# A graph network's node stages: two interleaved groups of tiles set half a chain apart

## Chip, core and metric

The kernel runs on one core of a Trainium2 chip. The metric is the device time of one execution in microseconds, lower is better; the median of three runs stands for a kernel. An engine (TensorE, VectorE, ScalarE, GpSimd, and SyncE for transfers) works through its own list of instructions in order; semaphores order the engines among each other.

## What is computed

A network of four layers on a graph of 6250 nodes and 100,000 edges. Each node has 64 scalars and 32 vectors of three components, 160 numbers. Each layer sends messages over the edges, sums them at the nodes, and ends with

```python
x = _layernorm(x + _L0_gnn_ref(x, ...), axis=-1)     # and so for layers 1, 2, 3
```

What a node does in between is small: projections of its 64 scalars and 96 vector components with small matrices, layer norms (mean, variance, `(variance + eps) ** -0.5`), a gate, in layer 0 a feed-forward part, and in layer 3 `cos(angle) * sc + sin(angle) * conv`. At the end of a layer the node's features are multiplied into the table (`tab_src`, and `tab_dst` for layers 0 and 2) from which the next layer's edges gather.

## The kernel before

The nodes are padded to 7168, or 56 tiles of 128. A *group* is `G = 4` tiles. `node_phase(nc, W, D, post, pre)` (line 2024) is the node stage between two edge stages: it ends layer `post` and prepares the tables of layer `pre`. It is called five times, with (None, 0), (0, 1), (1, 2), (2, 3) and (3, None); the edge stages (not touched) lie between. Each call loops `PAIRS = 7` times over two groups, `both`, which have their own buffers, PSUM and semaphores (`class Group`, line 1987). One pass of the loop is called a round here.

The work on a group is one chain: the list `stages` names its L steps in order (L is 12, 46, 35, 22 and 33 in the five calls), and the semaphore `B.done` counts them. A step waits until the step before it of the same group is done, whichever engine did that:

```python
def at(eng, name, B, j):
    eng.wait_ge(B.done, 1 + j * L + index[name])
```

On every engine each step is issued `for B in both`, that is for group 0 and then for group 1, before the next step. So the two groups go through the chain together, one step's length apart. In the steps, `turn_...` are transposes on TensorE (L2151, L2210), `move_...` copy their result out of PSUM on ScalarE (L2255, L2256), `product`, `f1`, `f2`, `tables` are matmuls (L2158, L2223, L2225), `..._mean` to `..._norm` is a layer norm, of which the step `..._root` is a power on GpSimd (L2137) and the rest is on VectorE, with the square on ScalarE. `move_t` writes the table's tile, `pair` takes the sums that the edge stage left.

In the calls (None, 0) and (0, 1) GpSimd has a second task, off the chain: it raises the edges' squared lengths, W["norm"], 784 columns, to the power -0.5, a seventh of them (112 columns) at the end of each round (L2142).

SyncE loads the sums of a group for the next round once the step `used` (`turn_a` or `move_v`) is reached, and stores tables or output when a group's chain is whole. There is one buffer of each kind for a group.

Of the kernel before, what the change touches and what calls it, by code (L numbers as in the profile page):

```python
# [17 lines left out]
ALU = mybir.AluOpType  # L18
# [3 lines left out]
P = 128  # L22
# [4 lines left out]
G = 4  # L27
PAIRS = -(-N_NODES // (P * 2 * G))
NT = PAIRS * 2 * G
# [332 lines left out]
def edge_tables(nc, W, D):  # L362
# [3 lines left out]
    with ExitStack() as ctx:  # L366
# [14 lines left out]
        GROUPS = ET // 16  # L381
        BATCH = 4
        batches = [range(a, min(a + BATCH, GROUPS)) for a in range(0, GROUPS, BATCH)]
# [1640 lines left out]
def node_phase(nc, W, D, post, pre):  # L2024
# [49 lines left out]
    with ExitStack() as ctx:  # L2074
        S = Names(nc, ctx, f"n{post}{pre}".replace("None", "x"))
        sem = S.sem
        both = [Group(S, n, post, pre, n_tab, H) for n in range(2)]
        X = lambda B, j: W["x"][:, bass.ds((j * 2 + B.n) * G, G), :]
        NA = lambda B, j: W["na"][:, bass.ds((j * 2 + B.n) * G, G)]
# [6 lines left out]

        @block.sync
        def _(sp):
            def load(B, j):
                if post == 1:  # L2090
                    for k in range(TM):
                        sp.dma_start(B.ag[k][:, :, :], rows(D["acc"][post][k][0:NPAD, :], j * 2 + B.n)).then_inc(B.loaded, 16)
                else:

                    for t in range(G):
                        slot = sp.value_load(W["last"][0:1, bass.ds((j * 2 + B.n) * G + t, 1)], min_val=0, max_val=V)
                        sp.dma_start(B.ag[0][:, t, :], D["sums"][post][bass.ds(slot, 1), :, :].rearrange("o p c -> (o p) c")).then_inc(B.loaded, 16)

            def store(B, j):

                if pre is not None:
                    for n, name in enumerate(("tab_src", "tab_dst")[0:n_tab]):
                        sp.dma_start(rows(D[name], j * 2 + B.n), B.tab[:, n, :, :]).then_inc(B.stored, 16)
                else:
                    sp.dma_start(rows(D["out"], j * 2 + B.n), B.final[:, :, :]).then_inc(B.stored, 16)
# [8 lines left out]
            with sp.Fori(1, PAIRS) as j:  # L2114
                if post is not None:
                    for B in both:

                        wait_apart(sp, B.done, 1 + (j - 1) * L + index[used], sem("sp_passed"))
                        load(B, j)
                for B in both:  # L2120

                    wait_apart(sp, B.done, 1 + j * L, sem("sp_passed"))
                    store(B, j - 1)
            for B in both:
                sp.wait_ge(B.done, 1 + PAIRS * L)
                store(B, PAIRS - 1)
# [3 lines left out]
        @block.gpsimd  # L2130
        def _(pool):
            with pool.Fori(0, PAIRS) as j:  # L2132
                for tag in ("ln2_", "end_", "pre_"):
                    if tag + "root" in index:
                        for B in both:
                            at(pool, tag + "root", B, j)
                            nc.gpsimd.tensor_tensor(B.st[:, :, :], B.st[:, :, :], W["half"][:, 0:2 * G].rearrange("p (a t) -> p a t", a=2), ALU.pow)\  # L2137
                                .then_inc(B.done, 1)
                if norms is not None:

                    share = norms[:, bass.ds(j * (ET // PAIRS), ET // PAIRS)]
                    nc.gpsimd.tensor_tensor(share, share, W["half"][:, 0:ET // PAIRS], ALU.pow).then_inc(sem("norms"), 1)  # L2142

        @block.tensor
        def _(pe):
# [19 lines left out]
            pe.wait_ge(sem("ones"), 2)  # L2165
            with pe.Fori(0, PAIRS) as j:
                if post in (0, 2):
                    for B in both:
# [3 lines left out]
                    for B in both:  # L2172
# [6 lines left out]
                if post == 0:  # L2179
                    for B in both:  # L2180
# [3 lines left out]
                    for B in both:  # L2184
# [3 lines left out]
                    for B in both:  # L2188
# [4 lines left out]
                    for B in both:  # L2193
# [3 lines left out]
                if post in (1, 3):  # L2197
                    per = 128 if post == 1 else 96
                    for B in both:
# [3 lines left out]
                    for B in both:  # L2203
# [3 lines left out]
                    for B in both:  # L2207
# [5 lines left out]
                    if post == 1:  # L2213

                        for B in both:
                            at(pe, "product", B, j)
                            times(B.wideB, 0, (B.aT[:, :], W["l1_out_s"][:, :]), (B.sT[0:64, :], W["l1_skip_s"][:, :])).then_inc(B.done, 1)
                        for B in both:
# [9 lines left out]
                    else:  # L2228

                        for B in both:  # L2230
# [5 lines left out]
                        for B in both:  # L2236
# [3 lines left out]
                if pre is not None:  # L2240
                    for B in both:
                        src = B.nrm if pre in (0, 2) else B.out
                        at(pe, "turn_p", B, j)
                        turn(src, 0, C0, B.psA)
                        turn(src, C0, CX, B.psA, SECOND).then_inc(B.done, 1)
                    for B in both:
                        at(pe, "tables", B, j)
                        times(B.wideB, 0, (B.sT[0:W[f"l{pre}_tab_s"].shape[0], :], W[f"l{pre}_tab_s"][:, :]))
                        times(B.wideA, 0, (B.vT[:, :], W[f"l{pre}_tab_v"][:, :])).then_inc(B.done, 1)

        @block.scalar
        def _(act):
# [5 lines left out]
            def square(tag, source, j):  # L2258
                for B in both:
                    src = source(B)  # L2260
                    at(act, tag + "square", B, j)
# [3 lines left out]
            with act.Fori(0, PAIRS) as j:  # L2265
                if post in (0, 2):
                    for B in both:
# [3 lines left out]
                if post == 0:  # L2271
                    square("ln2_", lambda B: B.res, j)
                    for B in both:
# [3 lines left out]
                    for B in both:  # L2277
# [5 lines left out]
                    for B in both:  # L2283
# [4 lines left out]
                    for B in both:  # L2288
# [4 lines left out]
                    for B in both:  # L2293
# [4 lines left out]
                if post in (1, 3):  # L2298
                    per = 128 if post == 1 else 96
                    for B in both:  # L2300
# [3 lines left out]
                    for B in both:  # L2304
# [3 lines left out]
                    for B in both:  # L2308
# [3 lines left out]
                if post == 1:  # L2312
                    for B in both:
                        at(act, "silu", B, j)
                        nc.scalar.activation(B.out[:, :, 0:C0], B.wideB[:, :, 0:C0], ACT.Silu).then_inc(B.done, 1)
                    for B in both:
                        at(act, "gate_t", B, j)
                        nc.scalar.activation(B.th[:, :, :], B.wideB[:, :, C0:96], ACT.Tanh, scale=0.5).then_inc(B.done, 1)
                if post == 3:

                    for B in both:
                        at(act, "sine", B, j)
                        nc.scalar.activation(B.whole_t[:, :, :], B.ang[:, :, :], ACT.Sin).then_inc(B.done, 1)
                if post is not None:
                    for B in both:
                        at(act, "end_square", B, j)
                        nc.scalar.activation(B.sqr[:, :, :], B.cen[:, :, :], ACT.Square).then_inc(B.done, 1)  # L2327
                if pre in (0, 2):
                    square("pre_", lambda B: B.out, j)
                if pre is not None:  # L2330
                    for B in both:
# [11 lines left out]
                    for B in both:  # L2343
# [6 lines left out]
                        last.then_inc(B.done, 1)  # L2350

        @block.vector
        def _(dve):
# [9 lines left out]
            def stats_eq(tag, source, j, dv, eps):  # L2363

                scalars, vectors = lambda B: source(B)[:, :, 0:C0], lambda B: source(B)[:, :, C0:CX]
                for B in both:
                    at(dve, tag + "mean", B, j)
                    reduce(B.st[:, 0, :], scalars(B)).then_inc(B.done, 1)
                for B in both:
                    at(dve, tag + "scale_mean", B, j)  # L2370
                    ts(B.st[:, 0, :], B.st[:, 0, :], -1.0 / C0, None, ALU.mult).then_inc(B.done, 1)
                for B in both:
                    at(dve, tag + "centre", B, j)
                    tt(B.cen[:, :, 0:C0], scalars(B), bcast(B.st[:, 0, :], 2, C0), ALU.add).then_inc(B.done, 1)
                for B in both:
# [3 lines left out]
                for B in both:  # L2379
# [3 lines left out]
                for B in both:  # L2383
# [6 lines left out]
            with dve.Fori(0, PAIRS) as j:  # L2390
                if post is not None:
                    for B in both:
# [6 lines left out]
                    if post == 1:  # L2399
                        for B in both:  # L2400
                            at(dve, "sum", B, j)
                            tt(B.ag[0][:, :, :], B.ag[0][:, :, :], B.ag[2][:, :, :], ALU.add).then_inc(B.done, 1)
                if post in (0, 2):
                    total = lambda B: B.ag[0][:, :, CX:CX + H]
                    for B in both:
                        at(dve, "denom", B, j)
                        ts(B.den[:, :, :], total(B), 1e-12 if post == 0 else 1e-16, None, ALU.add).then_inc(B.done, 1)
                    for B in both:
                        at(dve, "recip", B, j)
                        nc.vector.reciprocal(B.den[:, :, :], B.den[:, :, :]).then_inc(B.done, 1)  # L2410
                    if post == 0:
                        for B in both:
                            at(dve, "ratio", B, j)
                            tt(B.ratio[:, :, :], total(B), B.den[:, :, :], ALU.mult).then_inc(B.done, 1)
                    for B in both:
# [5 lines left out]
                if post == 0:  # L2421

                    for B in both:
# [3 lines left out]
                    for B in both:  # L2427
                        at(dve, "merged", B, j)
                        tt(B.nrm[:, :, 0:C0], B.nrm[:, :, 0:C0], B.cen[:, :, 0:C0], ALU.add).then_inc(B.done, 1)
                if post == 0:  # L2430
                    for B in both:
                        at(dve, "residual", B, j)
                        tt(B.res[:, :, :], X(B, j), B.wideB[:, :, 0:CX], ALU.add).then_inc(B.done, 1)
                    stats_eq("ln2_", lambda B: B.res, j, C1V, 1e-5)
                    for B in both:
# [3 lines left out]
                    for B in both:  # L2439
# [5 lines left out]
                    for B in both:  # L2445
# [3 lines left out]
                    for B in both:  # L2449
# [3 lines left out]
                    for B in both:  # L2453
                        at(dve, "both", B, j)
                        tt(B.out[:, :, :], B.out[:, :, :], B.res[:, :, :], ALU.add).then_inc(B.done, 1)
                    for B in both:
                        at(dve, "whole", B, j)
                        tt(B.res[:, :, :], B.out[:, :, :], X(B, j), ALU.add).then_inc(B.done, 1)
                if post == 1:
                    for B in both:  # L2460
                        at(dve, "gate_half", B, j)
                        ts(B.th[:, :, :], B.th[:, :, :], 0.5, 0.5, ALU.mult, ALU.add).then_inc(B.done, 1)
                    for B in both:
                        at(dve, "gated", B, j)
                        tt(comp(B.out[:, :, C0:CX]), comp(B.wideA[:, :, 0:C1V]), bcast(B.th[:, :, :], 2, 3), ALU.mult).then_inc(B.done, 1)
                    for B in both:
                        at(dve, "whole", B, j)
                        tt(B.res[:, :, :], B.res[:, :, :], B.out[:, :, :], ALU.add).then_inc(B.done, 1)
                if post == 2:

                    for B in both:
                        at(dve, "twice", B, j)
                        tt(B.out[:, :, :], B.res[:, :, :], B.wideB[:, :, 0:CX], ALU.add).then_inc(B.done, 1)
                    for B in both:
                        at(dve, "whole", B, j)
                        tt(B.res[:, :, :], B.res[:, :, :], B.out[:, :, :], ALU.add).then_inc(B.done, 1)
                if post == 3:
                    for B in both:
# [3 lines left out]
                    for B in both:  # L2482
# [3 lines left out]
                    for B in both:  # L2486
                        at(dve, "turns", B, j)
                        ts(B.whole_t[:, 0, :], B.ang[:, 0, :], 1.0 / (2 * PI), None, ALU.mult).then_inc(B.done, 1)
                    for B in both:
                        at(dve, "turns_i", B, j)  # L2490
                        nc.vector.tensor_copy(B.turns_i[:, 0, :], B.whole_t[:, 0, :]).then_inc(B.done, 1)
                    for B in both:
                        at(dve, "turns_f", B, j)
                        nc.vector.tensor_copy(B.whole_t[:, 0, :], B.turns_i[:, 0, :]).then_inc(B.done, 1)
                    for B in both:
# [11 lines left out]
                    for B in both:  # L2507
# [170 lines left out]
```

## Time and profile before

| | |
|---|---|
| time, three runs | 13734.82 us median (13729.59 to 13742.96) |
| the profiled execution | 13737.42 us, of which 13735.7 us from the first to the last instruction |
| TensorE, VectorE, GpSimd, ScalarE busy | 76%, 64%, 59%, 34% of the span |
| granted clock of TensorE, mean | 0.761 of 2.4 GHz |
| the five node stages (us from the start) | about 166 to 323, 3805 to 4370, 6960 to 7460, 11170 to 11415, 13397 to 13735 |

The page of the profile cuts the span into 40 slices of 343 us; a digit is a share in tenths. Line numbers (L2142) are those of the code above. A timeline row gives the start, the length from the first of its instructions to the end of the last, the engine, the line, what is written and read, and how many instructions (x8); an f32 matmul of this kernel shows as two. In brackets stands how long the engine was idle before it, and what ended that.

### The profile page before, as it was taken

What the parts mean: (1) busy time and instruction counts of PE and PEld (TensorE: products, weight loads), DVE (VectorE), ACT (ScalarE), POOL (GpSimd) and SP (SyncE); (2) the same over time, 40 slices, a digit from 0 to 9 for tenths busy, and PEclk for the clock granted to TensorE, in tenths of its full rate; (3) what the DMA queues carried; (4) which work ended last, traced back from release to release, by engine and by line L of the source; (5) the groups of instructions that cost most, each with busy time, mean ns of one, the idle gap of its engine ahead of it and who ended that gap; (6) DMA issues with size and microseconds to landing.
All of it is one profiled execution on the core that took longest, in us unless ns stands there. A gap on an engine that the chain in (4) does not pass through costs nothing. (4 is left out here: it accounts for less than half of the span.)

```text
span 13735.7 us, 242376 instructions
## 1 busy us (share of the span) xinstructions
PE 10467.3 (76%) x54203; PEld 8391.8 (61%) x54203; DVE 8817.4 (64%) x21902; ACT 4716.7 (34%) x11245; POOL 8106.9 (59%) x8692
## 2 busy tenths in 40 slices
PE   2999999937756666666655999999976767888885
PEld 2888888836654222222245999999975655555554
DVE  4677777775534555555534999999985445555553
ACT  1555555500022222222212777777750002222221
POOL 4788888825524888888822666666635534555540
PEclk7788888855556777777766999999975557888885
DMA  3454544424402888888852222222214532222221
GB/s 93 107 114 113 115 114 114 109 64 129 129 24 46 132 132 131 132 131 132 132 150 83 74 74 74 74 74 75 75 47 119 125 80 61 69 69 69 69 68 46
DMA packets 1339115, 1294.01 MB, mean 94 GB/s; under 512 B 504078, under 2 KB 1142018, under 8 KB 1338374
## 3 DMA queue, kind: packets, MB, share of 16 engines
q0 software_dynamic: 347904, 594.12, 23.4%
q1 hardware_dynamic: 913612, 653.03, 17.8%
q10 hardware_dynamic: 77498, 45.68, 1.1%
q8 instruction: 43, 0.70, 0.0%
q14 instruction: 58, 0.48, 0.0%
HBM read 781.38 MB, written 510.73 MB: 94 GB/s over the span
## 5 line engine op out<-in xcount | busy, mean ns | idle before, releaser
L625 POOL DMA_INDIRECT e_gs<-tab_src,e_ix x1568 | 1731.9, 1105 | 926.8 <-DMA e_ix<-in_dst 506.3
L625 POOL DMA_INDIRECT e_gd<-tab_dst,e_ix x1568 | 1620.6, 1034 | 478.0 <-issue 478.0
L676 PE MATMUL e_psS<-e_rows,e_same 128*128 128x480 f32 x1568 | 1120.1, 881 | 847.1 <-DVE e_same L650 847.1
L1391 PE MATMUL s_psS<-s_wv,s_hot 128*128 128x168 f32 (+1 forms) x3904 | 1183.0, 481 | 639.9 <-POOL s_wv L1349 357.8
L1602 POOL DMA_INDIRECT e_g<-tab_src,e_er x976 | 940.0, 963 | 963.6 <-DVE e_rows L1698 665.1
L1391 PEld LDWEIGHTS s_psS<-s_wv,s_hot 128*128 128x128 f32 x3904 | 1003.7, 316 | 818.6 <-issue 624.0
L694 POOL DMA_INDIRECT acc<-e_sums,e_row x784 | 1249.5, 1594 | 239.0 <-issue 209.7
L676 PEld LDWEIGHTS e_psS<-e_rows,e_same 128*128 128x128 f32 x1568 | 432.9, 294 | 1541.6 <-issue 1513.8
L581 PE MATMUL e_psF<-w_ident,e_F 128*128 128x128 f32 x7056 | 1343.0, 304 | 15.7 <-ACT e_FT L602 10.4
L608 ACT ACTIVATE e_O<-e_psO 128x352 f32<-128x352 f32 (+1 forms) x2352 | 1050.2, 447 | 768.6 <-PE e_psO L594 742.4
L602 ACT ACTIVATE e_FT<-e_psF 128x384 f32<-128x384 f32 x2352 | 1147.2, 488 | 307.4 <-PE e_psF L581 271.7
L581 PEld LDWEIGHTS e_psF<-w_ident,e_F 128*128 128x128 f32 x7056 | 938.6, 162 | 112.1 <-issue 56.6
L625 POOL DMA_INDIRECT e_g<-tab_src,e_ix x784 | 820.6, 1047 | 249.2 <-issue 175.2
L684 ACT ACTIVATE e_sums<-e_psS 128x480 f32<-128x480 f32 x784 | 447.8, 571 | 1509.7 <-PE e_psS L676 1509.7
L1626 PE MATMUL e_psS<-e_rows,e_hot 128*128 128x384 f32 x1952 | 941.0, 641 | 21.9 <-DVE e_hot L1700 12.3
L1347 POOL TENSOR_TENSOR s_wv<-s_val,s_pb 128x128 f32<-128x128 f32 x1464 | 776.8, 557 | 0.0
L1343 POOL TENSOR_TENSOR s_rel<-s_key,w_shift 128x4 int32<-128x4 int32 x488 | 98.0, 201 | 1142.1 <-DMA s_pb<-probs 1142.0
L2137 POOL TENSOR_TENSOR n_st<-n_st,w_half 128x8 f32<-128x8 f32 x70 | 113.4, 1638 | 1085.1 <-DVE n_st L2562 938.7
L593 PE MATMUL e_psO<-w_l_t,e_FT 128*128 128x128 f32 x3136 | 725.9, 317 | 0.0
L2255 ACT ACTIVATE n_sT<-n_psA 64x512 f32<-64x512 f32 x70 | 41.4, 591 | 1962.2 <-PE n_psA L2151 1960.9
L1626 PEld LDWEIGHTS e_psS<-e_rows,e_hot 128*128 128x128 f32 x1952 | 471.8, 254 | 360.5 <-issue 251.7
L591 PE MATMUL e_psO<-w_l_t,e_FT 96*128 96x128 f32 x3136 | 684.4, 304 | 2.0 <-ACT e_O L608 1.1
(481 smaller groups left out, 26530.6 us busy)
## 6 DMA issues: line engine op xcount, KB each, us to landing
s_val<-val SPq DMA_DIRECT2D x488, 320.0 KB
val<-e_O SPq DMA_DIRECT2D x392, 320.0 KB, 2.7
acc<-w_zeros SPq DMA_DIRECT2D x392, 139.5 KB
n_ag<-acc SPq DMA_DIRECT2D x56, 960.0 KB
e_krow<-in_src_t SPq DMA_DIRECT2D x196, 256.0 KB
sums<-e_total SPq DMA_DIRECT2D x244, 192.0 KB, 1.9
e_es<-in_es SPq DMA_DIRECT2D x196, 130.0 KB
e_gs<-tab_src,e_ix POOLq DMA_INDIRECT x1568
```

Source lines behind the costliest of these rows:

```text
L581: last = nc.tensor.transpose(psF[:, P * g:P * g + P], F[:, k, P * g:P * g + P], ident[:, :])
L591: nc.tensor.matmul(o[:, 0:scalars], f[0:96, 0:P], W[w + "_t0"][:, :], start=True, stop=True, skip_group_check=True)
L593: nc.tensor.matmul(o[:, x0:x0 + P], f[:, P:2 * P], W[w + "_t1"][:, :], start=False, stop=True, skip_group_check=True)
L602: nc.scalar.activation(FT[:, k, :], psF[:, 0:F_W], ACT.Copy).then_inc(S.sem(tag + "_FT"), 1)
L608: nc.scalar.activation(O[:, k, :], o[:, 0:width], ACT.Copy).then_inc(S.sem(tag + "_O"), 1)
L625: pool.indirect_dma_start(into[t][u][:, k, :], None, tables[t], bass.IndirectOffsetOnAxis(ix[u][:, t, k:k + 1], 0))\
L676: nc.tensor.matmul(psS[(k) % len(psS)], T["same"][u][:, k, :], values[:, k, :], start=True, stop=True)\
L694: pool.indirect_dma_start(acc[k], bass.IndirectOffsetOnAxis(T["row"][u][:, k:k + 1], 0), T["sums"][u][:, k, :], None, compute_op=ALU.add). ...
L1347: tt(wv[u][:, :, a:a + C1].rearrange("p t (h c) -> p t h c", h=H), val[u][:, :, a:a + C1].rearrange("p t (h c) -> p t h c", h=H), bcast(pb ...
L1391: last = nc.tensor.matmul(psS[u][:, 0:width], hot[u][:, k, :], wv[u][:, k, :], start=(k == 0), stop=(k == TM - 1))
L1602: pool.indirect_dma_start(g[u][:, k, :], None, D["tab_src"], bass.IndirectOffsetOnAxis(er[u][:, k, 12:13].bitcast(I32), 0))\
L1626: last = nc.tensor.matmul(psS[u % 2][:, 0:width], hot[u % 2][:, k, :], rows[u % 2][:, k, :], start=(k == 0), stop=(k == TM - 1))
```

## The change

All five calls. The two groups still alternate, but group 1 runs half a chain (`L // 2` steps) behind group 0. Each engine's list is written by `weave`: a step with index k of group B is put in slot `k + B.n * L // GROUPS`, taken modulo L, where the steps that overrun belong to the round before; in a slot, group 0 comes first. Steps that have no partner are peeled in front of the loop and behind it. The steps themselves, their waits and their buffers are the same. The power of W["norm"] is cut in smaller pieces, one behind each `root` step: 2 pieces of 56 columns a round in (None, 0), 4 of 28 columns in (0, 1). SyncE's list is put in the new order of events: for each group store (`whole`), then load (`free`).

```diff
+        offsets = [B.n * L // GROUPS for B in both]
+        def weave(eng, stream):
+            def turn(j, early, late):
+                runs = []
+                for B, offset in zip(both, offsets):
+                    runs += [[stream(B, j - 1), offset - L]] * early + [[stream(B, j), offset]] * late
+                for run in runs:
+                    run.append(next(run[0], None))
+                    while run[2] is not None and index[run[2]] + run[1] < 0:
+                        run[2] = step(run[0], False)
+                for slot in range(L):
+                    for run in runs:
+                        while run[2] is not None and index[run[2]] + run[1] == slot:
+                            run[2] = step(run[0], True)
...
+            turn(0, False, True)
+            with eng.Fori(1, PAIRS) as j:
+                turn(j, True, True)
+            turn(PAIRS, True, False)
...
-                        for B in both:
-                            at(pool, tag + "root", B, j)
...
-                    share = norms[:, bass.ds(j * (ET // PAIRS), ET // PAIRS)]
-                    nc.gpsimd.tensor_tensor(share, share, W["half"][:, 0:ET // PAIRS], ALU.pow).then_inc(sem("norms"), 1)
+            roots = [tag + "root" for tag in ("ln2_", "end_", "pre_") if tag + "root" in index]
+            share = ET // PAIRS // (len(roots) * GROUPS)
+            def stream(B, j):
+                for n, root in enumerate(roots):
+                    if (yield root):
+                        at(pool, root, B, j)
...
+                        if norms is not None:
+                            part = norms[:, bass.ds(((j * len(roots) + n) * GROUPS + B.n) * share, share)]
+                            nc.gpsimd.tensor_tensor(part, part, W["half"][:, 0:share], ALU.pow).then_inc(sem("norms"), 1)
+            weave(pool, stream)
...
-            with pe.Fori(0, PAIRS) as j:
+            def stream(B, j):
                 if post in (0, 2):
-                    for B in both:
+                    if (yield "turn_a"):
                         at(pe, "turn_a", B, j)
...
+            def free(B, j):
+                wait_apart(sp, B.done, 1 + j * L + index[used], sem("sp_passed"))
+                load(B, j + 1)
+            def whole(B, j):
+                wait_apart(sp, B.done, 1 + (j + 1) * L, sem("sp_passed"))
+                store(B, j)
...
+            with sp.Fori(1, PAIRS - 1) as j:
+                for B in both:
+                    whole(B, j - 1)
+                    if post is not None:
+                        free(B, j)
```

ScalarE's and VectorE's lists are rewritten as TensorE's is.

## Rows read from the trace of the kernel before

**Rows 1.** The page: span, and TensorE's busy tenths and granted clock by slices

```profile
span 13735.7 us, 242376 instructions
...
PE   2999999937756666666655999999976767888885
...
PEclk7788888855556777777766999999975557888885
```

**Rows 2.** Windows of one steady round in each of the five calls

```profile
core 0: us, PE busy (x) PEld busy (x) DVE busy (x) ACT busy (x) POOL busy (x), PEclk, DMA share, GB/s
172.30:193.80 21.50, 8.45 (x48) 7.48 (x48) 6.70 (x22) 7.09 (x16) 21.43 (x3) 0.66 0.20 61
3884.40:3963.70 79.30, 46.61 (x219) 40.96 (x218) 29.19 (x77) 20.96 (x52) 24.72 (x6) 0.59 0.06 17
7099.30:7170.30 71.00, 40.02 (x194) 34.96 (x193) 29.43 (x49) 16.14 (x34) 6.47 (x4) 0.59 0.36 129
11271.70:11306.25 34.55, 19.70 (x96) 17.20 (x96) 16.04 (x38) 7.29 (x14) 3.24 (x2) 0.55 0.14 39
13494.50:13539.80 45.30, 23.89 (x144) 22.34 (x144) 17.67 (x60) 8.13 (x16) 3.24 (x2) 0.61 0.17 50
```

**Rows 3.** Timeline of a round of (0, 1): single steps

```profile
3883.41 18.26 POOL L2142 TENSOR_TENSOR w_norm<-w_norm,w_half 128x112 f32 x1
...
3887.22 1.97 PE L2158 MATMUL n_psB<-w_l_tab_s,n_sT 64*128 64x64 f32 x8
...
3903.57 1.04 PE L2158 MATMUL n_psB<-w_l_proj_s,n_sT 65*128 65x64 f32 x8
...
3912.18 3.24 POOL L2137 TENSOR_TENSOR n_st<-n_st,w_half 128x8 f32<-128x8 f32 x2 [10.50 <-DVE n_st L2382]
...
3921.00 2.77 PE L2158 MATMUL n_psA<-w_l_f_v,n_vT 96*128 96x192 f32 x8
...
3924.18 1.15 ACT L2280 ACTIVATE n_sc<-n_psB,n_attr 128x128 f32<-128x128 f32 x4 [4.31 <-DVE n_attr L2438]
...
3930.32 1.77 ACT L2286 ACTIVATE n_th<-n_psB,n_attr 128x64 f32<-128x64 f32 x8
3931.89 2.69 ACT L2291 ACTIVATE n_fv<-n_psA,n_attr 128x192 f32<-128x192 f32 x8
3933.36 1.10 DVE L2443 SCALAR_TENSOR_TENSOR n_fv<-n_th,n_fv 128x256 f32<-128x256 f32 x3 [4.10 <-ACT n_fv L2291]
...
3943.23 0.42 DVE L2447 TENSOR_TENSOR n_out<-n_psB,w_l_f_b 128x256 f32<-128x256 f32 x1 [7.52 <-PE n_psB L2158]
...
3949.25 0.42 DVE L2447 TENSOR_TENSOR n_out<-n_psB,w_l_f_b 128x256 f32<-128x256 f32 x1 [5.14 <-PE n_psB L2158]
...
3950.06 1.55 DVE L2451 TENSOR_TENSOR n_out<-n_out,n_attr 128x640 f32<-128x640 f32 x2
...
3962.87 3.69 PE L2151 MATMUL n_psA<-w_ident,n_out 128*64 128x128 f32 x16 [13.65 <-DVE w_x L2571]
...
3964.79 0.59 ACT L2255 ACTIVATE n_sT<-n_psA 64x512 f32<-64x512 f32 x1 [6.33 <-PE n_psA L2151]
```

**Rows 4.** Timeline of a round of (1, 2): `pair`, and where `product` and `product_v` start

```profile
7099.28 2.16 DVE L2396 TENSOR_TENSOR n_ag<-n_ag 128x1920 f32<-128x1920 f32 x1 [6.35 <-ACT n_tab L2349]
...
7103.43 0.48 DVE L2398 COPY n_res<-w_x 128x640 f32 x1
...
7122.81 0.74 PE L2158 MATMUL n_psB<-w_l_out_s,n_aT 96*128 96x96 f32 x2
...
7128.17 0.74 PE L2223 MATMUL n_psA<-w_l_skip_v,n_vT 96*128 96x96 f32 x2
...
7135.02 0.72 PE L2223 MATMUL n_psA<-w_l_skip_v,n_vT 96*128 96x96 f32 x2
```

**Rows 5.** Timeline of a round of (3, None): the 24 small matmuls of `product`

```profile
13507.58 4.47 PE L2158 MATMUL n3x_psB<-w_l_w_v,n3x_gT 96*128 96x32 f32 x24
```

**Rows 6.** The instructions that write `w_norm`: count, shortest, median, longest in ns

```profile
L2142 POOL TENSOR_TENSOR w_norm<-w_norm,w_half x14: 18254/18258/18276, 175.6 to 4354.6; 128x112 f32 x14
```

More of the change, by code:

```diff
@@ L2113, in _ @@
                     load(B, 0)
-            with sp.Fori(1, PAIRS) as j:
-                if post is not None:
-                    for B in both:
-                        wait_apart(sp, B.done, 1 + (j - 1) * L + index[used], sem("sp_passed"))
-                        load(B, j)
-                for B in both:
-                    wait_apart(sp, B.done, 1 + j * L, sem("sp_passed"))
-                    store(B, j - 1)
-            for B in both:
-                sp.wait_ge(B.done, 1 + PAIRS * L)
-                store(B, PAIRS - 1)
+            def free(B, j):
[5 more added lines that the diff above has]
+            if post is not None:
+                for B in both:
+                    free(B, 0)
+            with sp.Fori(1, PAIRS - 1) as j:
+                for B in both:
+                    whole(B, j - 1)
+                    if post is not None:
+                        free(B, j)
+            for j in (PAIRS - 2, PAIRS - 1):
+                for B in both:
+                    whole(B, j)
             for B in both:
@@ L2228, in _ @@
                     else:
-                        for B in both:
+                        if (yield "product"):
                             at(pe, "product", B, j)
@@ L2271, in _ @@
                 if post == 0:
-                    square("ln2_", lambda B: B.res, j)
-                    for B in both:
+                    yield from square("ln2_", lambda B: B.res, B, j)
+                    if (yield "move_n"):
                         at(act, "move_n", B, j)
@@ L2328, in _ @@
                 if pre in (0, 2):
-                    square("pre_", lambda B: B.out, j)
+                    yield from square("pre_", lambda B: B.out, B, j)
                 if pre is not None:
-                    for B in both:
+                    if (yield "move_p"):
                         at(act, "move_p", B, j)
@@ L2389, in _, with stream @@
                 nc.vector.memset(B.sT[64:65, :], 1.0).then_inc(sem("ones"), 1)
-            with dve.Fori(0, PAIRS) as j:
+            def stream(B, j):
                 if post is not None:
-                    for B in both:
+                    if (yield "pair"):
                         at(dve, "pair", B, j)
@@ L2477, in _ @@
                 if post == 3:
-                    for B in both:
+                    if (yield "angle"):
                         at(dve, "angle", B, j)
```

206 lines of the change are left out of this document (104 added, 102 removed).

## Prediction

> **What bounds the kernel now.** The page first: one core, 13735.7 us from first to last instruction; the run that was profiled took 13737.42 us, 2.6 us above the median of the three timed runs (13734.82), so a difference worked out from the trace may be set on either. No engine is busy throughout, and the kernel is a row of stages. The change touches only the five calls of the node stage, so I looked for them in the instructions of the tiles `st`, `res` and `tab`, and then walked one steady round of each call in the timeline: a round is one pass of the loop over `PAIRS`, with two groups, and there are seven. The windows of one round each [rows 2] give everything: 21.5 us for the call before layer 0, 79.3 for (0, 1), 71.0 for (1, 2), 34.55 for (2, 3) and 45.3 for (3, None), together 251.65 us; seven times that is 1761 us, 12.8% of the kernel. The rest should not move.
>
> In four of the five rounds no engine is full: TensorE is busy 46.6 of 79.3 us, 40.0 of 71.0, 19.7 of 34.55 and 23.9 of 45.3 [rows 2]. These rounds are bound by the chain of dependent steps of a group, of which the other group hides a part. The exception is the first: GpSimd is busy 21.43 of 21.50 us. It raises 112 columns of `norms` to the power -0.5 each round, 18.26 us [rows 6], plus two `root` steps in 3.24 [rows 3].
>
> **Prices.** A step is taken as its duration plus 0.04 us where it follows on its own engine and about 0.1 where another engine hands over. VectorE over 640 columns: two groups in 1.55, so 0.86 alone. ScalarE: a move is two activations of 0.59, 1.2 with the handover; `scalars` 1.25, `gate_t` 0.95 and `gate_v` 1.4 (half of 1.77 and 2.69), `gated` 1.15. TensorE at its lower level (1.2 GHz): a `turn` 1.9 (two groups in 3.69), 8 matmuls of 64 columns 1.97, 8 of 192 columns 2.77, so `product` and `tables` of (0, 1) 3.95, `f1` 5.2; at the upper level (2.4 GHz) 1.04 in place of 1.97; `f2` 6.1 (its second group lies between 3943.2 and 3949.25) [all rows 3]. In (1, 2) `pair` is 4.65, `product` 5.4, `product_v` 6.9 [rows 4]; in (3, None) `product` is 1.97 + 4.47 = 6.4 [rows 3, 5]. With these, one chain alone at the lower clock is 60.5 us in (0, 1), 52.6 in (1, 2), 27.1 in (2, 3), 33.3 in (3, None).
>
> **What the change adds and moves.** No arithmetic goes or comes, apart from the cut of the `norms` power. Each engine's list is now in slots: group 0 is at stage k while group 1 is at k + L/2. All four engines work their lists in order, so an instruction of one group stands behind the one that the other has in an earlier slot, however late that is. Half a chain in *number of stages* puts these together. X is the group in the first half of its chain, Y the one in the second.
>
> (0, 1), L = 46, offset 23. Y: `scalars` to `f2` in slots 0 to 6 takes 1.25 + 0.95 + 1.4 + 1.15 + 2.9 + 1.6 + 6.1 = 15.35 us, in which X has only seven small VectorE steps (about 3 us). X's `turn_a` is slot 7, behind `f2` on TensorE: + 1.95 + 1.2 + 3.95, at 22.45. Both then stand in the statistics, on VectorE and ScalarE together: X's variance at 28.5. Both roots are in slot 17 (index 17 and 40): X's root 1.65, then the new piece of `norms` of 28 columns, then Y's root 1.65. The piece is priced by the slope between 8 columns in 1.64 and 112 in 18.26, 0.16 a column and 0.36 fixed: 4.85 us, put between the two roots; Y's root ends at 36.65. Y's `norm` 1.7 and `turn_p` 1.95: 40.3. X's `f1` is slot 21 and Y's `turn_p` slot 19 of one TensorE list, so `f1`, ready at 34.5, starts at 40.3 and ends at 45.4; Y's `tables` 3.9 and `move_t` 1.0: 50.3. X's `scalars` is slot 23, behind `move_t` on ScalarE. With the order inside a slot reversed (group 1 in the first half) the same walk gives 48.7. A round is 99.0 us at the lower clock.
>
> The clock gives some back. All TensorE work of this round at the lower level is 2 x 28.1 = 56.2 us (three turns 5.7, `product` 3.95, `f1` 5.2, `turn_f` 3.2, `f2` 6.1, `tables` 3.95); the trace has 46.6 [rows 2], so the upper level saved 9.6. I keep 85% of that, because TensorE's steps hold most, not all, of the new path: 99.0 - 8.2 = 90.8, a half of 45.4. The ends run alone: group 0's first half and group 1's second, together 60.5, 57 with the same share of clock. So 57 + 13 x 45.4 = 647 against 7 x 79.3 = 555: **+92**. Of it 7 x 9.7 = 68 us are the `norms` pieces, two a round on the path. They were hidden: the 18.26 us ran behind `end_root`, with no root wanted until the next `ln2_root`, 29 us after their start [rows 3].
>
> (1, 2), L = 35, offset 17. `pair` to `gate_half` of X is 4.65 + 2.15 + 3 x (2.0 + 1.2) + 5.4 + 6.9 + 1.1 = 29.8. Y has reached `pre_norm` at about 20, but that is slot 12 on VectorE behind X's `gate_half`; only then `norm` 1.0, `turn_p` 1.95, `move_p` 1.45, `tables` 4.8, `move_t` 1.7: 40.7. The other half is alike, 81.4 a round. Two chains of TensorE steps at the lower level (four turns 7.8, 5.4, 6.9, 4.8) are 49.8, the trace has 40.0 [rows 2]: the clock saves 9.8 now, 85% kept: 73.1. With ends of 50: 50 + 13 x 36.55 = 525 against 497: **+28**.
>
> (2, 3), L = 22, offset 11: X's `share` ready at 4.0 (behind Y's `sum`), `turn_a` 2.05, `move_a` 1.2, `product` 3.95, then Y's `turn_p` behind `product` on TensorE 1.95, `move_p` 1.2, `tables` 3.95, `move_t` and `tab_attr` 1.8: 20.1, or 40.1 a round; less 0.85 x (23.4 - 19.7) is 37.0. 26 + 13 x 18.5 = 266 against 242: **+24**.
>
> (3, None), L = 33, offset 16: X to the end of `product_v` 0.5 + 6.0 + 3.6 + 6.4 + 3.9 = 20.4; Y's `scale` stands behind X's `angle`, and its `centre`, `square`, `sum`, `var`, root and `norm` add 6.0: 26.4, or 52.8; less 0.85 x (32.6 - 23.9) is 45.4. 31 + 13 x 22.7 = 326 against 317: **+9**.
>
> First call: GpSimd still bounds. Two pieces of 56 columns cost one fixed part of 0.36 us more than one of 112: 7 x 0.36, **+3**.
>
> SyncE: the same loads and stores in the order in which they fall due (whole of group 0, its `used`, whole of group 1, its `used`). Each load is issued when its buffer is free, most of a chain ahead, so I cost it at nothing; were the loads of (1, 2) late, VectorE's `pair` would show it.
>
> Sum: 3 + 92 + 28 + 24 + 9 = +156 us, **13,890 us** (+1.1%).
>
> **A rule beside the rows.** What the clock will grant is the least certain term. In the page's slices TensorE's nines come with a granted 7 to 9, yet the rounds here, busy 59, 56, 57 and 53%, were granted 0.59, 0.59, 0.55 and 0.61 [rows 1, 2]. The Trainium skill ("TensorE: Matmul & The Clock Gate", Part 1) says that the clock rises with sustained work and falls back when the engine idles, and that such oscillation costs a kernel whose bursts are broken by waits. By that rule the change, which cuts the bursts of two groups into single ones, would push the clock down, and the sum would be nearer the first rival; by the rows it stays at 0.55 to 0.6.
>
> **The rivals.**
> 1. *The clock stays at its lower level* in the four calls. Then nothing is given back, at the ends neither (60.5 + 13 x 49.5 = 704 in (0, 1), and so on): 704 + 582 + 288 + 376.5 + 153.5 against 1761 is +343, 14,078 us. For it: single bursts; against: the share granted hardly varies over four different rounds. 0.15.
> 2. *The clock rises*, since some TensorE work is now nearly always there. At the upper level throughout, each half loses half its TensorE time: 36.55, 28.2, 14.1 and 18.2 us; with ends of 46.5, 40, 21 and 25 the sums are 522, 407, 204 and 262, and with the 153.5 of the first call -212, 13,523 us. It decides from the point where 343 of the 555 us between these two levels are given back, 62% of the work at the upper level; it is 32 to 53% now. 0.16, of which 0.08 ends within 0.2% of no change.
> 3. *The order doesn't bind* and the two chains overlap as in the idea: each call then takes seven and a half single chains, 454 + 395 + 203 + 250 = 1302 against 1611, and +3 in the first: 13,429 us. For it: TensorE and VectorE are free enough. Against: the slots above; it needs that two long TensorE steps don't meet. 0.08.
> 4. The forecast, 0.61, with a range of its own of 13,800 to 14,000 (the 85% taken as 50 to 100%, the `norms` piece costing half of what the slope says or all, and 0.1 us a handover either way).
>
> **Range and chances.** 13,740 to 14,080 leaves out rival 3 and the faster half of rival 2. Beyond 0.2% (27 us; closer than that this kernel's runs can't be told apart) faster: 0.08 + 0.08 = 0.16; within: 0.08; slower: 0.61 + 0.15 = 0.76.
>
> **What would show it.** Rounds of about 91, 73, 37 and 45 us in the timeline, GpSimd full in the first call with 9.3 us pieces; in (0, 1) the second root 6.5 us after the first, and `f1` released by nothing but the place behind `turn_p`; in (1, 2) VectorE idle before `pre_norm` until ScalarE's `gate_t`, long after its root. The granted clock of each call tells 1 and 2 apart from 4. I am wrong if rounds come near 65, 55, 30 and 36 us (the order doesn't bind), or if the time is made in another stage.

## The result

The changed kernel takes 14064.76 us, median of four runs (14042.80 to 14074.75); the kernel before took 13738.89 us in the four runs beside it. The ratio is 1.0233, with a 95% interval of 1.0215 to 1.0250: slower by 326 us, 2.4%. The forecast was slower by 156 us, 13,890, in a range up to 14,080. The direction and most of the mechanism held; the size is off by a factor of two, and it was off in one term. The first rival (TensorE's clock stays at its lower level) had put 14,078 us on it.

The profiled execution of the changed kernel spans 14041.1 us, 305.4 more than before. First, where: the windows of the whole node stages, each from the first to the last instruction of its call, in the order (None, 0), (0, 1), (1, 2), (2, 3), (3, None). Before:

```profile
core 0: us, PE busy (x) PEld busy (x) DVE busy (x) ACT busy (x) POOL busy (x), PEclk, DMA share, GB/s
165.80:322.70 156.90, 66.09 (x336) 58.72 (x336) 47.10 (x142) 49.66 (x112) 150.06 (x21) 0.61 0.19 58
3807.20:4373.50 566.30, 321.22 (x1512) 282.70 (x1512) 205.18 (x534) 147.12 (x364) 172.90 (x35) 0.58 0.06 17
6942.50:7456.60 514.10, 276.09 (x1344) 242.54 (x1344) 207.24 (x338) 112.30 (x238) 45.37 (x28) 0.60 0.35 125
11160.30:11413.00 252.70, 135.14 (x672) 118.10 (x672) 113.47 (x254) 51.00 (x98) 22.71 (x14) 0.55 0.13 37
13391.30:13734.90 343.60, 182.10 (x1008) 170.70 (x1008) 124.48 (x408) 57.25 (x112) 22.72 (x14) 0.58 0.16 46
```

After:

```profile
165.90:334.60 168.70, 89.20 (x336) 74.88 (x336) 48.34 (x142) 49.63 (x112) 152.55 (x28) 0.51 0.17 54
3815.70:4524.00 708.30, 387.77 (x1512) 328.98 (x1512) 214.67 (x534) 149.12 (x364) 178.60 (x56) 0.51 0.05 13
7092.80:7694.90 602.10, 349.48 (x1344) 292.04 (x1344) 218.56 (x338) 112.22 (x238) 45.84 (x28) 0.50 0.30 107
11382.80:11660.00 277.20, 158.41 (x672) 135.85 (x672) 118.59 (x254) 51.02 (x98) 24.31 (x14) 0.51 0.12 34
13642.20:14039.80 397.60, 232.79 (x1008) 206.11 (x1008) 133.22 (x408) 58.39 (x112) 22.93 (x14) 0.50 0.13 39
```

Read the length, the first busy time and the clock of each row. The stages are 11.8, 142.0, 88.0, 24.5 and 54.0 us longer, together 320. (The edge stages between them are 15 us shorter in this execution, nearly all of it behind (1, 2); the runs don't say why.) TensorE issues the same number of instructions, and is busy 237 us longer: its granted clock fell from 0.55 to 0.61 to 0.50 to 0.51, which is the lower level, 1.2 GHz, nearly without a break. In (2, 3) and (3, None) the added TensorE time, 23.3 and 50.7 us, is nearly all of the added length; in (1, 2) it is 73.4 of 88.0; in (0, 1) 66.6 of 142.0.

The loads that SyncE's new order sends are not late: in (1, 2) VectorE's `pair` waited for a transfer once, 11.6 us, against twice, 16.5 us in all, before.

The rest of (0, 1) is seen in the timeline of one round of the changed kernel:

```profile
3992.78 0.17 DVE L2481 COPY n_attr<-w_na 128x4 f32 x1 [11.20 <-PE n_psA L2198]
...
4011.18 1.94 PE L2198 MATMUL n_psB<-w_l_proj_s,n_sT 65*128 65x64 f32 x8 [1.25 <-ACT n_vT L2297]
...
4020.82 1.64 POOL L2176 TENSOR_TENSOR n_st<-n_st,w_half 128x8 f32<-128x8 f32 x1 [35.43 <-DVE n_st L2426]
4022.42 4.79 POOL L2180 TENSOR_TENSOR w_norm<-w_norm,w_half 128x28 f32 x1
...
4027.18 1.64 POOL L2176 TENSOR_TENSOR n_st<-n_st,w_half 128x8 f32<-128x8 f32 x1
...
4030.58 1.89 PE L2191 MATMUL n_psA<-w_ident,n_out 128*64 128x128 f32 x8 [5.14 <-DVE w_x L2615]
4032.26 2.77 PE L2198 MATMUL n_psB<-w_l_f_s,n_sT 65*128 65x192 f32 x8
...
4037.52 1.97 PE L2198 MATMUL n_psB<-w_l_tab_s,n_sT 64*128 64x64 f32 x8
...
4037.73 0.17 DVE L2481 COPY n_attr<-w_na 128x4 f32 x1 [7.29 <-PE n_psA L2198]
...
4090.99 0.17 DVE L2481 COPY n_attr<-w_na 128x4 f32 x1 [11.20 <-PE n_psA L2198]
```

L2481 is the step `attr`, behind `f1`: from 3992.78 to 4090.99 a round is 98.2 us; 99.0 was worked out for the lower clock. The second root starts 6.4 us after the first, with the piece of 28 columns between them (4.79 us; forecast 4.85). `f1` at 4032.26 had its inputs at 4026.8 and stood behind the other group's `turn_p`, which the late root had held up; `tables` stands behind `f1`. And `product` takes 1.94 us for 8 matmuls that took 1.04 in [rows 3].

In (1, 2) the wait is the one forecast: Y's variance is ready at 7320.2 (its root takes 1.7 us more), and its `pre_norm` (L2429) starts at 7331.86, behind X's `gate_half` (L2506), which waited for ScalarE:

```profile
7319.99 0.16 DVE L2426 TENSOR_SCALAR n_st<-n_st 128x4 f32<-128x4 f32 x1
7331.72 0.23 DVE L2506 TENSOR_SCALAR n_th<-n_th 128x128 f32<-128x128 f32 x1 [11.56 <-ACT n_th L2360]
7331.86 0.42 DVE L2429 TENSOR_TENSOR n_nrm<-n_cen,n_st 128x256 f32<-128x256 f32 x1
```

In (None, 0) GpSimd isn't quite full any more: from 249 us on it waits 1.8 us before every other root, 7.2 us in all. The likely reason is that the chain is longer at the lower clock, 0.51 in place of 0.61; no run separates the two.

```profile
238.47 9.28 POOL L2180 TENSOR_TENSOR w_norm<-w_norm,w_half 128x56 f32 x1
249.55 1.64 POOL L2176 TENSOR_TENSOR nx_st<-nx_st,w_half 128x8 f32<-128x8 f32 x1 [1.79 <-DVE nx_st L2426]
```

### The profile page after: what moved, and what is told of

Its sections match the earlier page's. It is cut to its first block and busy times, and to the rows that moved or that the text cites. A ratio compares the mean times of both kernels' runs of the same rounds, so it can differ in the third digit from the quotient of the medians.

```text
span 14041.1 us, 242566 instructions
## 1 busy us (share of the span) xinstructions
PE 10673.8 (76%) x54203; PEld 8543.4 (61%) x54203; DVE 8853.6 (63%) x21902; ACT 4718.0 (34%) x11245; POOL 8106.2 (58%) x8720
```

## The experiments

Theory A: the loss is two things, TensorE's clock, which the new order keeps low, and the pieces of W["norm"] between two roots. Against it stand B (the lists block by themselves, whatever the clock), C (the rewriting of the lists costs) and D (the clock is granted in the same share in any case, so the order is to blame). The first four kernels ran on a chip where the kernel before takes 16,338 us. There is no trace of it from that chip, but in `e3_off0_whole`, which does the same work in nearly the same order, the node stages take 1848 us (1834 before), and nearly all of the difference lies in the edge stages. So the runs are compared by stage length, and by the ratio to the kernel before on the same chip. Stage lengths and clocks are from one execution each; the same code differed by up to 19 us in (0, 1) and 9 us in the other calls between two executions, so smaller differences between them decide nothing.

**Pieces undone.** `e1_piece_whole`:

```diff
-                        if norms is not None:
-                            part = norms[:, bass.ds(((j * len(roots) + n) * GROUPS + B.n) * share, share)]
+                        if norms is not None and B.n == GROUPS - 1 and n == len(roots) - 1:
+                            part = norms[:, bass.ds(j * (ET // PAIRS), ET // PAIRS)]
...
```

> The changed kernel with one part undone: the power of W["norm"] is again one piece of 112 columns a round, behind the last root of group 1; the half-chain order stays. Theory A (two losses: TensorE's clock, which the new order keeps at its lower level, and the pieces between the two roots): a round of (0, 1) loses 2 x 4.8 us, from 98.2 to 88.6, so 14,065 - 67 = 13,998 us, and the granted clock stays at 0.50 to 0.51 in the node stages. Theory B (the in-order lists bind by themselves, the pieces are covered by the wait behind the other group's turn_p): less than 20 us, above 14,045.

Windows of its first two calls:

```profile
166.30:366.30 200.00, 90.98 (x336) 76.65 (x336) 48.98 (x142) 49.64 (x112) 150.44 (x21) 0.50 0.15 46
4279.30:4916.30 637.00, 364.53 (x1512) 309.74 (x1512) 215.47 (x534) 149.14 (x364) 172.89 (x35) 0.54 0.05 15
```

(0, 1) loses 71.3 us (708.3 to 637.0), as A has it (67). But its clock is 0.54 and not the 0.50 to 0.51 that A expected, and 23 of the 71 are TensorE's busy time, so 48 are the pieces' beside the clock. `e9_half_fill_late` below has the same (0, 1) code: 631.9 us, TensorE busy 359.5, and again 48. And (None, 0) grows by 31: there a piece of 18.25 us holds up a root of the other group, which two of 9.3 don't. The ratio is 1.0175 (1.0138 to 1.0212). The small pieces cost one call and helped another; the three other calls are the same within 2 us.

**Offset undone, pieces kept** (`offsets = [0, 0]`):

> The changed kernel with offsets [0, 0]: both groups at the same step, as before, but the power of W["norm"] in the small pieces of the change. Theory A: the clock returns to 0.58 to 0.60 in the four later calls; what stays is the pieces, 4.8 us before the second root, twice a round of (0, 1): +67 us, 13,806, and +3 in the first call. Theory B: all of the loss came with the offset, so within 20 us of 13,739.

(0, 1) is 647.5 us at 0.55, the four calls' clocks are 0.55 to 0.60 again, and (1, 2) to (3, None) take 513.4, 252.4 and 341.5 us, as before. The ratio is 1.0096 (1.0066 to 1.0127), which leaves out B, and also A's number (13,806 is 1.0049): the pieces cost more here than A said. In the first call they cost 59 us (215.8, at a clock of 0.50 in place of 0.61; 20 of the 59 are TensorE's busy time), against the 3 expected: with both groups at the same step, the second root has to wait for the first one's piece of 9.3 us. The price was right and its place was not.

**Both undone** (`offsets = [0, 0]`, one piece):

> Offsets [0, 0] and the power of W["norm"] in one piece: what is left of the change is how the lists are written (two peeled turns, SyncE's order). Theory A and B both: 13,739 within 15 us, clock 0.56 to 0.61. A third theory (C: the peeled turns and SyncE's new order cost by themselves) would have 10 us or more on each of the five calls, 13,790 and above.

The ratio is 0.9992 (0.9963 to 1.0022); the stages are 156.7, 572.2, 520.6, 255.1 and 343.4 us. C falls: the peeled turns and SyncE's order cost nothing that can be measured.

**One step apart** (`offsets = [0, 1]`, one piece):

> Offset of one step in place of half a chain, one piece of W["norm"]. The groups still work next to each other, so by theory A TensorE's stretches stay long and the clock at 0.58 to 0.60; and the steps in which both groups want the same engine at once (tables on TensorE, both norms on VectorE) come a little apart: at least as fast as before, 13,640 to 13,745. Theory B (any offset chains one group to the other's place in the lists): slower, 13,800 or more.

The ratio is 0.9925 (0.9885 to 0.9965). The stages are 156.0, 520.4, 505.4, 246.0 and 334.2 us, clocks 0.61, 0.61, 0.59, 0.54 and 0.58. An offset as such doesn't cost; B falls in this form.

**Other distances**, one run each, all with one piece, and the windows that matter below:

> Offsets of 11, 9, 4 and 14 steps in the four later calls (1 in the first), one piece of W["norm"]. Walked through with the prices of the rows and TensorE at its lower clock, the rounds add up to stages of 620, 560, 277 and 400 us; with a fifth of TensorE's time saved, as the groups next to each other get it, 545, 490, 244 and 355. Theory A says which: distance between the groups means the lower clock, 0.50 to 0.53, and the first numbers. Theory D: 0.57 to 0.60, and the second.

> Offsets of 3, 3, 2 and 2 steps in the four later calls (1 in the first), one piece of W["norm"]. The groups' steps on TensorE still follow each other closely. Theory A: clock 0.57 or above, stages within 4% of those with an offset of one step (520.4, 505.4, 246.0 and 334.2 us). Theory B (the farther apart, the more the lists block): each stage longer than with one step by 5% or more.

> Offsets of 2, 2, 3 and 3 steps in the four later calls. Theory A reads each stage by its clock: where it is granted 0.57 or more the stage is no longer than before (566, 514, 253, 344 us), where it is 0.52 or less it is longer than before by 5% or more. A stage with a clock of 0.57 or more that is still 5% longer than before, or one at 0.52 that is shorter, speaks against it.

| offset: stage us, TensorE busy us, clock | (0, 1) | (1, 2) | (2, 3) | (3, None) |
|---|---|---|---|---|
| 0 (before) | 566.3, 321.2, 0.58 | 514.1, 276.1, 0.60 | 252.7, 135.1, 0.55 | 343.6, 182.1, 0.58 |
| 1 (e4) | 520.4, 309.1, 0.61 | 505.4, 278.9, 0.59 | 246.0, 140.9, 0.54 | 334.2, 182.6, 0.58 |
| 2 (e11, e8) | 632.8, 376.0, 0.53 | 507.4, 295.2, 0.56 | 288.2, 155.8, 0.51 | 330.1, 175.1, 0.59 |
| 3 (e8, e11) | 627.9, 385.2, 0.52 | 528.9, 312.5, 0.54 | 277.9, 155.8, 0.51 | 362.4, 196.9, 0.55 |
| 11, 9, 4, 14 (e7) | 625.3, 384.8, 0.51 | 513.7, 305.1, 0.55 | 267.8, 159.5, 0.50 | 395.9, 232.8, 0.50 |
| half (e1) | 637.0, 364.5, 0.54 | 602.0, 349.6, 0.50 | 279.0, 160.1, 0.50 | 397.4, 232.8, 0.50 |

From one step to half a chain every stage gets longer at a lower clock, and TensorE's busy time is 55.5 of 116.6 us, 70.7 of 96.6, 19.2 of 33.0 and 50.2 of 63.2, between half and four fifths. The clock isn't all: (2, 3) is 288.2 us at an offset of 2 and 267.8 at 4, at the same low clock, and (1, 2) at an offset of 9 is no longer than before although TensorE is busy 29 us more. There the order seems to give back what the clock took. The expectations held where A says lower clock: 625.3, 267.8 and 395.9 against 620, 277 and 400. They missed in (1, 2) at an offset of 9: 513.7 at 0.55, between the two numbers. And they missed in `e8_off_small` in three calls of four: with the groups only two or three steps apart, (0, 1), (1, 2) and (2, 3) have 0.52, 0.54 and 0.51, and (0, 1) and (2, 3) are 21% and 17% longer than with one step, which is what B expected. (B missed in the two others: 4.6% longer and 1.2% shorter.) So "next to each other" isn't what keeps the clock. `e11_off_2233` decides little: by its rule only (2, 3) is decided (0.51, 10% longer than before, as A has it). (0, 1) at 0.53 is 12% longer, (1, 2) at 0.56 is 1.3% shorter and (3, None) at 0.55 is 5.5% longer, all between the two limits.

The clock can be compared without any change of order, too. `e4` and `e10` (below) run the same (0, 1) code: 520.4 us, TensorE busy 309.1, at 0.61 in one execution, and 501.5, busy 289.8, at 0.66 in the other. The stage is 18.9 us shorter, and TensorE's time 19.2. The other calls with the same code agree: (2, 3) at one step is 8.7 us shorter in `e10` than in `e4`, TensorE's time 8.6; (3, None) at two steps is 4.9 shorter in `e10` than in `e8`, TensorE's time 5.3; (2, 3) at half a chain is 7.4 shorter in `e5` (271.6 us at 0.52) than in `e1`, TensorE's time 7.4. With the code held, the stage pays nearly all that a lower clock adds to TensorE's time. This is the strongest evidence that the clock makes the length.

**The clock raised with the order kept.** `e5_half_fill` and `e6_off0_fill` put work for TensorE into a gap of (0, 1), both with one piece of W["norm"]. The edit of `e5` is shown; `e6` has offsets [0, 0] and fills behind group 1's product alone.

```diff
                         times(B.wideB, C0, (B.vT[:, :], W[f"l{post}_proj_v"][:, :])).then_inc(B.done, 1)
+                        if post == 0:
+                            for _ in range(32):
+                                nc.tensor.transpose(B.psA[:, 0:P], ident[:, :], ident[:, :])
```

> The half-chain order with one piece of W["norm"], and in the call (0, 1) 32 transposes of the identity behind every product, into a PSUM tile that nobody reads then: about 7 us of work for TensorE in a gap of 8.5 us, which adds nothing to the result. Read by the stage (0, 1), 637.0 us at a granted 0.543 without it. Theory A (the clock falls because the new order breaks TensorE's work into shorter stretches): the clock of the stage rises to 0.60 or more and f1, tables and f2 get shorter, 560 to 625 us. Theory D (the clock is given in about the same share whatever TensorE does in these stages, and the order is to blame): clock within 0.02 and 635 to 650 us.

> The same filling (32 transposes behind the product of group 1) with both groups at the same step, where the stage (0, 1) took 572.2 us at 0.578. The gap there is 7.5 us. Theory A: the clock rises above 0.60 and the stage is 520 to 565 us. Theory D: clock within 0.02, 570 to 590 us.

The window of (0, 1) in `e5_half_fill`, and in a second block a row of its timeline, a real transpose step at the upper level:

```profile
3860.50:4490.20 629.70, 424.48 (x1960) 373.35 (x1960) 215.50 (x534) 148.90 (x364) 172.89 (x35) 0.62 0.06 15
```

```profile
4003.12 1.03 PE L2191 MATMUL n_psA<-w_ident,n_out 128*64 128x128 f32 x8 [3.59 <-DVE w_x L2618]
```

The clock rose to 0.62 from 0.54, as A has it, and the stage fell by 1.1% against `e1` and by 0.3% against `e9`, which has the same code without the filling (631.9 us); neither theory had that. Of TensorE's 424.5 us the filling took 77.3, so that the real steps took 347.2 in place of 364.5 in `e1` and 359.5 in `e9`. The timeline says why: the upper level fell partly on the filling (32 transposes in 5.05 us here, 5.93 elsewhere), and on one pair of `f1` and `tables` (1.49 and 1.07 us for the first halves at 4007.38 and 4005.41), while the next pair at 4045.49 ran 2.77 and 1.97. In `e6_off0_fill` the clock went from 0.58 to 0.59 and the stage from 572.2 to 577.3. These are D's numbers and not A's. As a test of what the clock is worth it says little, since the filling (27.8 us) didn't raise it; the real steps took 331.0 us in place of 325.8.

`e9_half_fill_late` does it in the last two calls, behind `product_v` in (3, None) (the first part, with a wait until the PSUM tile is free) and behind `tables` in (2, 3):

```diff
+                            k = j if B.n else j - 1
+                            if not isinstance(k, int) or k >= 0:
+                                wait_apart(pe, both[1 - B.n].done, 1 + k * L + index["mix_b"], sem("pe_passed"))
+                                for _ in range(24):
+                                    nc.tensor.transpose(both[1 - B.n].psA[:, 0:P], ident[:, :], ident[:, :])
...
+                        if post == 2:
+                            for _ in range(24):
+                                nc.tensor.transpose(both[1 - B.n].psA[:, 0:P], ident[:, :], ident[:, :])
```

> The half-chain order with one piece of W["norm"], and in the calls (2, 3) and (3, None) 24 transposes of the identity, into a PSUM tile of the other group that is free then: behind tables in the first, behind product_v in the second. They add nothing to the result and fill gaps of about 6 us, so that TensorE works nearly without a break. The order of the real steps is that of the changed kernel, whose stages took 277.2 us at 0.506 and 397.6 us at 0.515. Theory A (the clock, not the order, makes these stages long): the granted clock rises above 0.60, the real TensorE steps get shorter, and the stages come to 235 to 265 and 330 to 375 us. Theory D (the order is to blame): the clock may rise or not, but the stages stay within 3%, 270 to 285 and 386 to 409 us.

The windows of the changed kernel above have the two clocks as 0.51 and 0.50.

Windows of the two calls, and in a second block TensorE in the timeline of (2, 3) (the first three rows) and of (3, None):

```profile
11345.10:11599.80 254.70, 191.07 (x1008) 174.56 (x1008) 118.63 (x254) 51.04 (x98) 24.30 (x14) 0.67 0.13 37
13591.30:13987.80 396.50, 285.57 (x1320) 259.16 (x1320) 133.34 (x408) 58.39 (x112) 22.93 (x14) 0.56 0.14 40
```

```profile
11422.43 1.07 PE L2198 MATMUL n_psB<-w_l_proj_s,n_sT 64*128 64x64 f32 x8 [1.25 <-ACT n_vT L2305]
11423.43 1.13 PE L2198 MATMUL n_psB<-w_l_proj_v,n_vT 96*128 96x96 f32 x8
...
11440.83 1.97 PE L2198 MATMUL n_psB<-w_l_proj_s,n_sT 64*128 64x64 f32 x8
...
13793.32 1.94 PE L2198 MATMUL n3x_psB<-w_l_w_s,n3x_aT 96*128 96x65 f32 x8 [1.25 <-ACT n3x_vT L2305]
...
13804.15 4.39 PE L2284 MATMUL n3x_psA<-w_ident 128*128 128x128 f32 x24
```

In (2, 3) the clock rose from 0.51 to 0.67, and `product` of one group runs at the upper level (1.07 and 1.13 us; at 11440.83 it still takes 1.97). Without the filling's 63.7 us TensorE was busy 127.4 us in place of 158.4, and the stage is 254.7 us in place of 277.2, with 336 more instructions in it: A's range. Here, in the half-chain order, the clock is shown to be the cause. In (3, None) the clock rose to 0.56, not above 0.60, and the stage stayed at 396.5, in D's range and not A's. The row at 13793.32 shows the reason: the steps on the chain still run at 1.2 GHz, and the upper level was reached in the filling alone (24 in 4.39 us, where a rate of 8 in 1.9 would be 5.7). Without the filling's 56.5 us TensorE was busy 229.1 us, against 232.8. So A was not put to the test there: the clock of the chain's steps hardly rose.

**The shortest of each**, offsets 1, 1, 1, 1 and 2 steps and one piece:

> The offsets that were shortest so far for each call: 1, 1, 1, 1 and 2 steps, one piece of W["norm"]. Sum of the stages from the two runs with them 156.0 + 520.4 + 505.4 + 246.0 + 330.1 = 1758 against 1834 in the kernel before: -76 us, ratio 0.9945 on a chip where the kernel before takes 13,740 us. Theory B (any offset costs): 1.00 or above.

Windows of its four later calls:

```profile
3809.60:4311.10 501.50, 289.82 (x1512) 253.63 (x1512) 210.12 (x534) 149.00 (x364) 172.91 (x35) 0.66 0.07 19
6883.20:7387.90 504.70, 278.49 (x1344) 245.06 (x1344) 211.95 (x338) 114.03 (x238) 45.38 (x28) 0.59 0.36 127
11102.20:11339.50 237.30, 132.30 (x672) 115.50 (x672) 116.53 (x254) 51.02 (x98) 22.71 (x14) 0.56 0.14 39
13322.00:13647.20 325.20, 169.78 (x1008) 157.09 (x1008) 128.22 (x408) 57.94 (x112) 22.95 (x14) 0.60 0.16 48
```

13649.03 us against 13749.72 for the kernel before on the same chip, ratio 0.9922 (0.9908 to 0.9935): 101 us faster (76 were expected), the fastest version of this study. Length less TensorE's busy time shows what the small offset itself gives in (0, 1): 245.1 us before, 211.7 here and 211.3 in `e4`.

## Why the prediction was wrong in size

**The walk through the lists was right.** At the lower clock it gave rounds of 99.0, 81.4, 40.1 and 52.8 us; measured are 98.2, 81.9, 37.6 and 54.5. The waits that it named are in the trace: `f1` behind `turn_p`, `tables` behind `f1`, `pre_norm` behind `gate_half`. Two of its prices are too low: `f2` at 6.1 us and the 24 matmuls at 4.47 were taken as prices of the lower level, but ran in part at the upper one. In the changed kernel they take 7.1 us (4051.50 to 4058.60) and 5.27. The second of these, 0.8 us twice a round, is nearly the whole difference in (3, None); the first would have made the round of (0, 1) 101, so part of that agreement is luck.

**The step that failed is "the clock gives some back ... I keep 85% of that".** I took the time that the upper level saved in a round before (9.6, 9.8, 3.7 and 8.7 us) and kept 85% of it. The 85% was for the share of the path that is TensorE's; that the clock would go on being granted as before rested only on its hardly varying over four rounds. It varied with the order: nearly none was kept. The term was 0.85 x 7 x 31.8 = 189 us of recovered time in the four calls; with 0 in its place, the sum is the first rival's +343, and +326 was measured, at a granted 0.50 to 0.51. Four rounds of one kind of order are no evidence on another kind. The Trainium skill ("TensorE: Matmul & The Clock Gate", "HAM oscillation — how this bites in real kernels") warns that waits between bursts bring the clock down. The fall from 0.58 to 0.51 in (0, 1) agrees with that in direction only: the longest wait of TensorE in a round was 13.65 us before [rows 3] and is 8.85 (before 4074.25) in the round of the changed kernel read above, so that longer waits are not the reason. I had given the rival 0.15.

**By call**, forecast and measured: +3 and +11.8; +92 and +142.0; +28 and +88.0; +24 and +24.5; +9 and +54.0. With nothing given back the walk has +149, +85, +46 and +59 for the four later calls. (2, 3) agrees with the forecast because two errors cancel: the walk was about 2.5 us a round too long, and the clock's share was 3.1 us too generous.

**The pieces of W["norm"]** were 68 us in (0, 1) by the forecast; undoing them gave 71.3, 48 of it beside the clock. In (None, 0) the forecast had them bound by GpSimd at +3; it was +11.8, with GpSimd waiting for the chain. Undoing them there costs 31 more, so that on the whole kernel they are 40 us, not 71.

**A slip in the second rival.** Half of (0, 1) without half of TensorE's 28.1 us is 35.45 us, not 36.55; the rival is then -226 us and not -212, and decides from 60% of the work at the upper level, not 62%. The forecast doesn't use it.

**What the half chain itself did.** Length less TensorE's busy time, with one piece: 245.1 to 272.5 us in (0, 1), 238.0 to 252.4 in (1, 2), 117.6 to 118.9 in (2, 3), 161.5 to 164.6 in (3, None). So even with TensorE's time left out, half a chain gained nothing in any of these four. Other distances did: 211.7 us in (0, 1) at one step, 208.6 in (1, 2) at nine, 108.3 in (2, 3) at four. The subtraction treats all of TensorE's time as if it lay on the path, so these are indications and not a proof.

**Open.** What of a list decides the clock in a stage isn't settled. Distance isn't it: (0, 1) falls to 0.53 at two steps, (3, None) not before three, (1, 2) keeps 0.55 at nine. And filling raised the clock in three calls, but made the real steps clearly shorter in (2, 3) alone. For (0, 1), (1, 2) and (3, None) no run clearly raised the clock of the chain's steps in the half-chain order; there the clock's part rests on TensorE's busy time and on the runs of the same code.

## What to carry to other kernels

Where a stage is a chain through several in-order engines, a second chain must be placed by what each list then has in front of a step, and walking the two lists by hand predicted the rounds here to within 7%. The prices for it must come from steps that ran wholly at one clock level. Before a reordering, work the sum out at both levels of TensorE's clock: the order that spreads its work evenly may be the one that runs all of it at the lower level. An optional piece of work on an engine of the chain must fit before the next step that either chain wants from it: 4.79 us between two roots cost (0, 1) 48 us and more, and 18.25 us behind a root cost (None, 0) 31 us.

## What the runs showed of the hardware

The granted clock of (0, 1) moved between 0.51 and 0.66 with the order of the same instructions (0.61 and 0.66 for the same code in two executions), and that of (2, 3) between 0.50 and 0.67, the 0.67 with work of no use added. Nor did a busy TensorE secure it: in (3, None) with filling it was busy 285.6 of 396.5 us, and the steps on the chain ran at 1.2 GHz. Transposes run at either level like matmuls: 8 in 1.89 us (4030.58 in the changed kernel), where all steps near it were at the lower level, and 8 in 1.03 us (4003.12 in `e5_half_fill`). A power on GpSimd took 1.64 us for 8 columns, 4.79 for 28, 9.28 for 56 and 18.26 for 112.
